# A binary-convolution and mixture-of-experts block: the block addition on GpSimd waits for one more piece of VectorE's routing

## The reference

```python
out1 = conv3x3(sign(ln_c(x) + move1), sign(w3) * scale)      # binary convolution
out1 = rprelu(ln_c(x) + bn(out1))
out2 = conv1x1(sign(out1 + move2), sign(w_pw) * scale)
out2 = rprelu(bn(out2) + out1)
x = x + out2                                                  # the block addition
t = to_tokens(x)                                              # 32 * 3136 tokens of 64 numbers
h = ln_t(t)
probs = softmax(h @ gate_w + gate_b)                          # 8 experts, one per token
expert, place = argmax(probs), running_count_of_the_expert    # place < capacity, else dropped
t = t + probs[expert] * (relu(h @ w1[expert] + b1) @ w2[expert] + b2)
```

## Time and profile before

| | us |
|---|---|
| runs of the kernel before | 2075.05, 2082.57, 2087.02 |
| median | 2082.57 |
| the profiled execution | 2080.89 |
| its span, first to last instruction | 2079.0 |
| mean granted TensorE clock in it | 0.881 of full speed |

### The profile page before, as it was taken

One profiled execution on the slowest core, in us unless ns is written; L12 is line 12 of the kernel. 1 busy time (PEld: TensorE's weight loads), 2 busy tenths in 40 slices (PEclk: granted clock), 3 DMA queues, 4 the chain that ended last, 5 costly groups with the idle time before them and its releaser, 6 DMA issues.

```text
span 2079.0 us, 40865 instructions
## 1 busy us (share of the span) xinstructions
PE 1654.2 (80%) x10341; PEld 880.9 (42%) x10341; DVE 1482.2 (71%) x3641; ACT 1206.3 (58%) x4066; POOL 1048.5 (50%) x1052
## 2 busy tenths in 40 slices
PE   7998888888888878775058888888888888878884
PEld 1344433443333434443034444555555445445453
DVE  3488878878887878888135666787677777777675
ACT  3687877777777877765035554655455454455451
POOL 2116655655676656667524444554444444444442
PEclk7898989988899989886579999999999999999896
DMA  9136766554557554442164555777777677777786
GB/s 240 40 97 145 176 165 157 150 142 117 148 149 135 139 133 108 108 112 78 59 191 142 145 147 144 193 219 244 226 234 230 220 236 225 228 222 228 227 247 221
DMA packets 302207, 351.64 MB, mean 169 GB/s; under 512 B 48452, under 2 KB 252452, under 8 KB 295940
## 3 DMA queue, kind: packets, MB, share of 16 engines
q1 hardware_dynamic: 260644, 264.23, 47.2%
q0 software_dynamic: 41120, 85.81, 13.3%
q10 hardware_dynamic: 320, 0.33, 0.1%
HBM read 179.70 MB, written 180.01 MB: 173 GB/s over the span
## 4 chain that ended last, share of the span: by engine, by line
PE 37%; issue 16%; DVE 14%; another core or an unknown queue 11%; POOL 8%; ACT 6%; DMA 4%; SPq 2%; ACTq 1%; POOLq 0%; DVEq 0%
PE bank L821 9%; PE bank L831 8%; POOL pairs_by_group L490 6%; PE bank L812 3%; PE bank L730 3%; POOL X L484 3%; PE bank L692 2%; PE bank L839 2%; PE bank L789 2%; PE bank L740 2%; DMA X<-weights_by_group 2%; PE bank L763 2%; ACT X L975 2%; DVE Z L1250 1%
## 5 line engine op out<-in xcount | busy, mean ns | idle before, releaser
L521 POOL DMA_INDIRECT results_by_pair<-X,PAIRNO x462 | 461.2, 998 | 542.1 <-ACT X L980 420.6
L490 POOL DMA_INDIRECT pairs_by_group<-ROWS,idx x400 | 435.4, 1088 | 133.2 <-issue 113.9
L821 PE MATMUL bank<-X 64*128 64x256 f32 x1848 | 287.7, 432 | 60.6 <-issue 28.7
L975 ACT ACTIVATE X<-bank,X 128x256 f32<-128x256 f32 x693 | 284.6, 474 | 76.2 <-PE bank L821 58.9
L968 ACT ACTIVATE X<-bank 128x256 f32<-128x256 f32 x231 | 90.5, 392 | 389.9 <-remote 238.1
L484 POOL TENSOR_TENSOR X<-Z,X 128x448 f32 (+1 forms) x112 | 137.0, 1223 | 308.9 <-DVE Z L1266 290.9
L831 PE MATMUL bank<-X 128*64 128x256 f32 x1848 | 276.3, 424 | 6.9 <-ACT X L985 6.9
L812 PE MATMUL bank<-ident,X 128*64 128x128 f32 x1848 | 159.3, 294 | 145.5 <-DMA X<-weights_by_group 69.2
L821 PEld LDWEIGHTS bank<-X 64*128 64x128 f32 x1848 | 180.3, 200 | 114.7 <-issue 103.3
L730 PE MATMUL bank<-S,WB 128*128 128x448 bf16 x1008 | 227.9, 374 | 0.0
L1289 DVE TENSOR_SCALAR X<-bank,X 128x256 f32<-128x256 f32 x231 | 111.1, 481 | 131.8 <-PE bank L821 63.3
(11 more groups left out here) (209 smaller groups left out, 3006.5 us busy)
## 6 DMA issues: line engine op xcount, KB each, us to landing
X<-weights_by_group SPq DMA_DIRECT2D x231, 258.5 KB
X<-pairs_by_group SPq DMA_DIRECT2D x231, 134.0 KB
pairs_by_group<-PAD SPq DMA_DIRECT2D x15, 1742.0 KB
X<-in_x_dram SPq DMA_DIRECT2D x16, 1568.0 KB
block_output<-X SPq DMA_DIRECT2D x112, 224.0 KB, 1.9
ROWS<-block_output SPq DMA_DIRECT2D x16, 1568.0 KB
Z<-results_by_pair SPq DMA_DIRECT2D x16, 1568.0 KB
out_dram<-ROWS SPq DMA_DIRECT2D x16, 1568.0 KB
```

The costliest lines, as they stand in the source:

```text
L490: pool.indirect_dma_start(rows, bass.IndirectOffsetOnAxis(ap=idx[0:m, p.odd, k:k + 1], axis=0), ROWS[0:m, p.odd, k, :], None).then_inc(s_s ...
L521: pool.indirect_dma_start(done, bass.IndirectOffsetOnAxis(ap=PAIRNO[:, u, j:j + 1], axis=0), RES[:, u, j, :], None,).then_inc(s_back[u], 16)
L821: mm(hidden(q), WR[b, ring, q // 2 * P:(q // 2 + 1) * P], XT[b, ring % 2, :], start=True, stop=True).then_inc(s_h, 1)
L975: last = A(HB[:, ring % 2, q, :], hidden(q), ACT.Relu, bias=WR[:, ring, at:at + 1])
```

## The change

POOL's block addition gets one more wait in front of it, in every chunk but c = 1: for the third piece of the routing, behind L1266. In chunk 3 it waits for `route(rou, 4)` and not for the slice of L1212 behind it; in chunk 4 it waits for the two slices; in chunk 6 the count is reached with L1178. Nothing is removed, no other engine's program changes, and there is no new instruction on any engine but POOL's wait, its register work and its `sem_inc`.

```diff
+            def vector_clear(c, rou, old):
+
+                if old and c == 0:
+                    wait_apart(pool, s_rr, old.n + 1)
+                if rou and c == 2:
+                    wait_apart(pool, s_sh, rou.n + 1)
+                if rou and c in (3, 5, 6):
+                    wait_apart(pool, s_route, rou.n * NROUTE + ROUTE_AT[{3: 5, 5: 11, 6: 14}[c]])
+                if rou and c == 4:
+                    wait_apart(pool, s_sl, rou.n * SLICES + SLICES - 1)
+
             def add_block(p, j):
 
                 wait_apart(pool, s_q2, p.n * NCH + j + 1)
@@
                         scatter_tiles(sca, (c - 1) * TILES // (NCH - 1), c * TILES // (NCH - 1))
                     if late:
+                        vector_clear(c, rou, sca)
                         add_block(late, j)
```

## The result

The changed kernel takes 2097.9 us in the median of 11 runs (2083.4 to 2112.4), the kernel before on the same chip 2078.1 (2067.9 to 2090.4). The ratio is 1.0081, 95% interval 1.005 to 1.0113: slower by some 17 us.

What follows compares the result with a forecast made beforehand. No engine was taken as saturated; they wait for each other in turn. Terms summed to +0.4 us per pass, +5 in twelve full passes, plus 2 at the edges: 2080.9 + 7 = 2088 us, 8-in-10 range 2064 to 2108.

Steps and rivals of the forecast that it cites:

- The sign: Whole kernel: slower with the change, by 7 us or 0.26%.
- the delay: From the end of the piece waited for to the addition's start: 0.65 us, bounded by 0.08 and 1.08.
- the holding: VectorE operations held by POOL's addition: at most 27 us to give back in ten passes, 2.7 per pass.
- within 0.5%: Whole kernel: the change does what it says and little comes of it, between 2072 and 2093 us; chance 0.45.
- second rival: PE starved by late blocks, or more often at 1.2 GHz: above 2093 us, 2107 with 1.08 us delay; chance 0.33.
- chunk 0: Addition starts 1.0 us later in the mean behind L1266 while PE idles for it: +1.0 us per pass.
- first rival: VectorE was the bound and is now free: below 2072 us, 2062 if the addition starts 0.08 us behind; chance 0.22.
- Chunk 4: Addition ends 0.8 us later, PE's wait for it weighted one in three: +0.3 us per pass.
- Chunk 5: Addition starts 1.27 us later, 0.8 is slack before PE's row product, 0.5 remains: +0.25 us per pass.
- Chunks 2 and 3: L1102 and L1119 give back 0.88 and 0.9 us, less new holding: -0.15 and -0.7 us per pass.
- Chunk 6: Small VectorE operations held less, -0.5 us per pass; PE's rows later, +0.2.
- The edge term: At the edges, above all in pass 1, the addition comes later by the piece's length: +2 us.

Runs made afterwards that it cites:

- the run with two more: The changed kernel with two more waits, both met long before, behind the new one; ratio 1.0163 against the kernel before.
- the reordered version: The changed kernel with all new waits kept, each put behind the three old waits instead of in front; ratio 0.9977 against the kernel before.

## Why the forecast was off

The sign held, and of the mechanism the delay and the holding; how much of a lateness is passed on did not. The forecast was +7 us and "within 0.5%" the likeliest, at 0.45; measured are +17 us, above the 2093 us where the second rival, PE starved by late blocks (0.33), begins, and under that rival's 2107. The range of 2064 to 2108 holds the result, in part by luck: four of the terms below miss by 0.6 to 1.1 us per pass, and not all in one direction.

**The delay.** Taken as 0.65 us. Measured 0.63 in chunk 5, and 0.89 and 0.62 in chunk 0 by pass of a turn. Right; the second rival's 1.08 was not the cause. Each wait behind the one met last costs by these runs 0.10 us (0.20 for the two of the run with two more) to 0.15 (0.45 for the three that the reordered version puts in front; 0.34, 0.11 each, in the other pass of a turn). Register work is in that, and for all but one of them (`s_tr`) an increment. The Trainium skill (Advanced Engine Details and Errata, Network/Comms) gives 50 to 100 ns for a sequencer's reading of a semaphore alone; no run here separates that reading from the rest. The forecast's estimate by that figure was 3 us less for 0.12 us less delay; by its own terms, 3.5 us per pass for one of delay, it is 5.

**What the holding gives back.** L1102, L1119 and L1201 went to 575, 186 and 186 ns, L1106 to 1213, all as forecast, and no addition of chunk 4 in passes 4 to 13 takes 2.06 us (1.13 in the mean). Not seen: L1135, 75 columns with both operands in SBUF, went from 281 to 776 ns. Over the program VectorE still got 35 us back, which the first rival would have turned into a gain.

**The terms, per pass.**

| chunk | forecast | alone, measured | addition later |
|---|---|---|---|
| 0 | +1.0 | +1.1 | 1.14 |
| 2 and 3 | -0.85 | -0.3 | 1.46 and 1.12 |
| 4 | +0.3 | +1.2 | 1.43 |
| 5 | +0.25 | +1.3 | 1.14 |
| 6 | -0.3 | -1.1 | 2.63 |
| sum | +0.4 | +2.2 | |
| 4, 5 and 6 in one run | +0.25 | +2.1 | |
| all together | | +1.4 | |

Three steps failed, all in how much of a slip is passed on.

Chunk 4: "I give this place one in three." Its addition ended 1.4 us later and not 0.8 (and by the forecast's own numbers 662.69 + 0.65 + 1.13 is 664.47 and not 664.6, 0.65 later), and a cost of about that size arrived. I had counted the waits of one engine, and taken a place without a wait for slack. A later addition makes a wait where there was none (26 places became 40), and the product behind it feeds a VectorE operation that already waited; that the whole cost comes over this link is the reading that fits best, and is not shown by a run of its own.

Chunk 5: "so 0.8 is slack and 0.5 remains." The slack was read from a single pass. By the run of this chunk alone nothing of it is left for the pass: 1.14 us of lateness, +1.3 of time. The way is not shown. The scatters queued behind the addition were named in the forecast and priced at nothing; the next addition is 0.84 us late behind them.

Chunks 2 and 3: "I count on PE's other idle time for that, and 2 us more if it isn't there." It was there in part: VectorE's 0.87 and 0.91 us less 0.52 for L1106 would make -1.3, and -0.3 came (-0.75 to +0.2).

Chunk 6 erred the other way: the holding was sized rightly (0.48 us), but the piece also waits less at L1151, 0.8 us.

Did the forecast give the delay too little weight? The runs on the order of the waits don't show that. Its terms give 3.5 us per pass for one of delay (+1.9 at 1.08 less -1.6 at 0.08). The reordered version saved 22 us (1.0081 less 0.9977, of 2078), by the two intervals 12 to 31; two more waits cost 17, by theirs 5 to 29. The delay of 0.33 us less at 3.5 makes 14 us, and 0.20 more makes 8. If the four additions that start on a wait (chunks 0, 2, 5 and 6) pass it on in full, reordering saves (0.40 + 0.40 + 0.33 + 0.33) x 12 = 18 us. All these fit. The delay was right and its weight is not refuted; what failed are the terms of chunks 4 and 5, which the reordered versions pay as well.

**PE's wait for the addition** was forecast at 45 us and is 77.3; the pass at 58 give or take one, and is 59.7 in that long execution. The edge term of 2 us was not tried.

**The clock.** It isn't needed for a loss: the version with chunk 4 alone loses 0.7% at an unchanged clock. For all waits together it stays open how much it adds; 0.003 less at 0.5 to 1.0 us per 0.001 is an estimate of 2 to 3 of the 17 us. In the eleven runs of the changed kernel the mean is 0.878, in the one profiled execution of before 0.881, and the changed kernel's profile shows the drop only behind 640 us (0.84 and 0.85 in 640 to 760 and 760 to 880, for 0.91 twice).

**Open.** The places don't simply add. The five parts alone sum to +2.2 us per pass where all together give +1.4, which their intervals allow; but chunk 0, chunks 2 and 3, and chunks 4 to 6 in one run sum to 1.75%, and the two halves with the new wait last to 0.7%, where the whole has 0.8% and -0.2%, in both cases some 0.9% less than its parts and just outside the intervals. One thing that moves between versions is the holding of L1102 (1808 ns with the waits of chunks 4 to 6, 1611 with chunk 4's, 575 with all), so a part can be charged for holding that the whole doesn't have; how much of the 0.9% that is stays open. Open, too, is why waits already met come out 0.4% faster. And why VectorE's L1151 starts 2.3 us behind the end that the profile gives for PE's product (663.90 + 0.69 to 666.92, timeline after): the end of a matmul is modelled, and no run here tells that from a late signal.

## What to carry to other kernels

A wait that keeps one engine's instruction off another's shared port paid here where many small operations were shielded and the delayed result had slack (chunk 6), and lost where the piece waited for is long and little in it was held (chunks 4 and 5). So try it place by place, and then in groups, for the places don't add: the version with three of the six places ran at 0.991 and that with the other three at 1.0155, and all six in the same order at 0.998. Put the wait that will be satisfied last at the end of the row, because whatever stands behind it delays the operation, wherever that starts on this wait and not on its engine's own queue (chunk 3): reordering alone took 1% off. And count a slip of a link between engines in full at each place unless several passes show idle time behind it; the number of waits that the profile lists there now was a poor guide (chunk 4).

## What the runs showed of the hardware

- A GpSimd wait with a count in a register, its increment included, took 0.10 to 0.15 us here; three of them (one without the increment) behind the last signal made 0.89 us of 0.44, in the other pass of a turn 0.62 of 0.28. Ahead of it they took nothing that can be measured: with the new waits long met the addition began 0.59 us behind L1266 in chunk 0 (0.66 before) and 0.47 in chunk 4 (0.47).
- What one engine holds moves on. The addition let go of L1102 (1447 to 575 ns) and took L1106 (563 to 1213) and L1135 (281 to 776); with 0.4 us less delay L1106 was held only to 810. An addition that started 0.41 us ahead of L1118 and ran 1.12 us held it until 0.44 us behind its own end (645.73 to 646.17), as L1102 was held before until 0.45 behind it. The Trainium skill (SBUF — State Buffer, SBUF: two separate sides) says that of a GpSimd operation and a VectorE operation with two SBUF inputs the one that starts first has the shared ports for its whole instruction and the other is blocked. The trace agrees.
- With 0.001 less mean granted clock an execution of the kernel before took 0.5 us more among 32 runs on one chip and 1.0 us more among 26 on another. That is how the two went together; no run here shows which of them causes the other.
